# A four-layer graph network: how many columns TensorE gathers per chunk, and which memory the running sums are scanned into

## The reference

```
x += h + segment_sum(h[src] * pattern, dst) / max(deg, 1)            # layer 1
x += h + softmax attention over each node's incoming edges           # layer 2
x += segment_sum(h[src], dst) @ W                                    # layer 3
x += segment_sum(tensor product of h[src] with sh0, sh1, sh2, dst)   # layer 4
```

## Time and profile before

| | us |
|---|---|
| median of three runs | 13893.11 |
| the profiled execution | 13869.06 |
| its span, first to last instruction | 13867.2 |
| busy: PE, DVE, ACT, POOL | 11075.0, 11170.5, 3293.7, 11498.1 |
| mean granted TensorE clock | 0.895 |

### The profile page before, as it was taken

How to read it: one execution, slowest core, us unless ns; L and a number is a source line. 1 busy time by engine, 2 the same in 40 slices (tenths; PEclk the granted TensorE clock), 3 DMA queues, 4 the chain that set the end, 5 groups by cost and what they waited for, 6 DMA issues and landing times.

```text
span 13867.2 us, 198598 instructions
## 1 busy us (share of the span) xinstructions
PE 11075.0 (80%) x49235; PEld 8972.2 (65%) x49235; DVE 11170.5 (81%) x15127; ACT 3293.7 (24%) x3628; POOL 11498.1 (83%) x19996
## 2 busy tenths in 40 slices
PE   7999999991666666666569999899859999999995
PEld 6888888881545554554458888888836666666663
DVE  8988989984999999999877777777757777777775
ACT  2222222220333333333222222222201111111110
POOL 6888888887888888888778888888878888888887
PEclk9999999995777777777789999999979999999997
DMA  3323333331232322223222222222222222222221
GB/s 106 86 82 94 94 94 91 81 86 37 73 84 71 83 76 81 77 77 80 57 65 66 67 70 70 71 68 67 62 45 50 57 50 55 52 55 53 55 53 34
DMA packets 863909, 963.05 MB, mean 69 GB/s; under 512 B 426441, under 2 KB 678253, under 8 KB 863105
## 3 DMA queue, kind: packets, MB, share of 16 engines
q1 hardware_dynamic: 396088, 456.93, 12.1%
q0 software_dynamic: 327744, 170.03, 8.6%
q10 hardware_dynamic: 139400, 330.44, 6.2%
HBM read 614.57 MB, written 341.90 MB: 69 GB/s over the span
## 4 chain that ended last, share of the span: by engine, by line
issue 48%; POOL 47%; DVE 2%; POOLq 1%; PE 1%; DMA 0%; ACT 0%; SPq 0%; DVEq 0%; ACTq 0%
POOL rows L418 33%; POOL work L423 11%; POOL outs L432 2%; POOLq L422 1%; POOL q_edges L397 1%; PE psum L554 0%; PE psum L631 0%; DVE work L935 0%; DVE work L937 0%; POOLq L416 0%; PE psum L592 0%; DVE rows L767 0%; DVE h_parts L710 0%; DMA idx<-src_c 0%; DVE work L703 0%
## 5 line engine op out<-in xcount | busy, mean ns | idle before, releaser
L418 POOL DMA_INDIRECT rows<-h_table,idx x9750 | 9651.2, 990 | 2093.0 <-POOL work L423 1701.5
L554 PE MATMUL psum<-h_parts,one_hot 128*128 128x448 f32 x38808 | 8674.5, 384 | 681.4 <-ACT one_hot L461 669.9
L554 PEld LDWEIGHTS psum<-h_parts,one_hot 128*128 128x128 f32 x38808 | 7609.7, 198 | 1582.1 <-issue 790.1
L461 ACT ACTIVATE one_hot<-bit_hot 128x896 fp32r<-128x896 bf16 x2177 | 2057.8, 951 | 6984.1 <-DVE bit_hot L740 6943.8
L761 DVE TENSOR_TENSOR tile_rows<-psum,h_mask 128x448 f32<-128x448 f32 x2772 | 1721.1, 621 | 925.5 <-PE psum L554 720.9
L631 PE MATMUL psum<-work,bd_t 128*128 128x512 f32 (+1 forms) x4500 | 1766.9, 521 | 191.6 <-DVE work L1133 110.8
L767 DVE TENSOR_REDUCE rows<-tile_rows 128x32 f32<-128x448 f32 x2772 | 1694.0, 611 | 0.0
L631 PEld LDWEIGHTS psum<-work,bd_t 128*128 128x128 f32 x4500 | 823.2, 196 | 915.0 <-issue 596.9
L423 POOL MEMSET work<- 128x32 f32 x9750 | 1404.0, 144 | 3.6
L1118 DVE TENSOR_TENSOR work<-psum,work 128x800 f32<-128x800 f32 x1125 | 1102.7, 989 | 318.5 <-PE psum L622 250.0
L740 DVE TENSOR_TENSOR bit_hot<-keys,target 128x896 bf16<-128x896 int16 x2177 | 1343.6, 617 | 11.0 <-issue 11.0
(11 more groups left out here) (176 smaller groups left out, 6020.9 us busy)
## 6 DMA issues: line engine op xcount, KB each, us to landing
rows<-h_table,idx POOLq DMA_INDIRECT x9750
sums<-outs ACTq DMA_DIRECT2D x375, 400.0 KB, 2.4
dwin<-keep_rows SPq DMA_DIRECT2D x1500, 100.0 KB
attn<-outs ACTq DMA_DIRECT2D x125, 800.0 KB, 3.4
dwin<-dst_w SPq DMA_DIRECT2D x500, 100.1 KB
edge_in<-pattern_c SPq DMA_DIRECT2D x125, 400.0 KB
q_edges<-work ACTq DMA_DIRECT2D x25, 2000.0 KB
edge_in<-q_edges SPq DMA_DIRECT2D x125, 400.0 KB
```

Source lines behind the costliest of these rows:

```text
L418: nc.gpsimd.indirect_dma_start(out=rows[:, r, j * D:(j + 1) * D], out_offset=None, in_=h_table[:, :], in_offset=bass.IndirectOffsetOnAxis( ...
L461: nc.scalar.activation(one_hots[i % TILE_BUFS[l]][:, :, :], bit_hots[i % BIT_BUFS[l]], ACT.Copy).then_inc(one_hot_cast, 1)
L554: last = nc.tensor.matmul(banks[TILE_BANKS[l][b]][:, 0:H0 * D], one_hots[b][:, h1, :], h_parts[:, part, h1 * H0 * D:(h1 + 1) * H0 * D], st ...
```

## The change

Four things change. The table `PE_COLS` goes from 4 to 6 columns per chunk in the second loop, from 7, 7, 7, 7, 8 to 8 in the third and from 4, 3, 4, 3, 4 to 4 in the fourth; GpSimd's counts fall to match (2625 to 2375, 2225 to 2125, 2675 to 2625 fetches; 9750 to 9350 in all). `BIT_BUFS` is 2 for the third loop. In the first three loops the running sum whose transpose goes out is scanned into PSUM and transposed from there; in the second loop `mz` too is made in PSUM, the last element of the sum is saved in a column `o_last`, the two transposes change places, `mz_ready` is signalled by the first of them, and the two added picks stand after them; ScalarE casts their successors after it has issued the store. In the fourth loop a line picks the tiles of `ahead` beyond the fourth; with four columns there are none.

```
@@ -52,9 +52,9 @@
...
 
-PE_COLS = ((7, 7, 7, 7, 8), (4,) * RING, (7, 7, 7, 7, 8), (4, 3, 4, 3, 4))
+PE_COLS = ((7, 7, 7, 7, 8), (6,) * RING, (8,) * RING, (4,) * RING)
 PE_MAX = max(max(c) for c in PE_COLS)
-BIT_BUFS = (3, 2, 3, 2)
+BIT_BUFS = (3, 2, 2, 2)
 TILE_BUFS = (3, 2, 4, 2)
...
@@ -195,6 +195,8 @@
...
         in_ps, qh_ps = wide[0:2]
+        total_ps = wide[1]
+        o_last = sb("o_last", [P, 1])[:, :]
         acc = psum[:, 6 * 512:8 * 512].rearrange("p (a c) -> p a c", a=2)
...
@@ -504,8 +506,9 @@
...
                     nc.scalar.activation(acc_wide, mx[:, 1:CH + 1], ACT.Copy, scale=half[:, 0:1]).then_inc(mz_m_ready, 1)
-                    cast_next(1, t, r, range(2, PE_MAX))
+                    cast_next(1, t, r, range(2, 4))
                     store(1, t, r, attn_chunks, 2 * CH)
+                    cast_next(1, t, r, range(4, PE_MAX))
             for q in range(PIECES):
...
@@ -826,7 +829,7 @@
...
 
-            link(nc.vector.memset(last_of(O), 0.0))
+            link(nc.vector.memset(last_of(total_ps), 0.0))
             pick_first(0)
...
@@ -858,10 +861,10 @@
...
                     v.wait_ge(edge_used[r], t + (1 + START))
-                    then(nc.vector.tensor_tensor_scan(O, keep, in_ps, last_of(O), ALU.mult, ALU.add))
+                    then(nc.vector.tensor_tensor_scan(total_ps, keep, in_ps, last_of(total_ps), ALU.mult, ALU.add))
                     pick_next(0, t, r, range(4, 5))
                     v.wait_ge(outs_stored[r], t * 16 + (0 * TURNS * 16 + START))
-                    nc.vector.transpose(outs[:, r, 0:CH], by_edge(O)).then_inc(outs_ready[r], 1)
+                    nc.vector.transpose(outs[:, r, 0:CH], by_edge(total_ps)).then_inc(outs_ready[r], 1)
                     pick_next(0, t, r, range(5, PE_MAX))
...
@@ -968,11 +971,11 @@
...
             nc.vector.memset(mx[:, 0:1], -BIG)
-            for total in (qh_ps, Z, O):
-                link(nc.vector.memset(last_of(total), 0.0))
+            for total in (last_of(qh_ps), last_of(Z), o_last):
+                link(nc.vector.memset(total, 0.0))
             pick_first(1)
             steps1 = steps[0]
-            per_chunk1 = 7
+            per_chunk1 = 6
             with v.Fori(0, TURNS) as t:
...
@@ -1002,23 +1005,26 @@
...
                     nc.vector.tensor_tensor(acc_wide, acc_wide, nb, ALU.subtract).then_inc(rise_ready, 1)
-                    pick_next(1, t, r, range(2, PE_MAX))
+                    pick_next(1, t, r, range(2, 4))
 
...
                     then(nc.vector.tensor_tensor(in_ps, in_ps, hT, ALU.mult))
-                    then(nc.vector.tensor_tensor_scan(O, u, in_ps, last_of(O), ALU.mult, ALU.add))
+                    then(nc.vector.tensor_tensor_scan(in_ps, u, in_ps, o_last, ALU.mult, ALU.add))
 
                     v.wait_ge(mz_m_ready, n)
-                    then(nc.vector.tensor_copy(mx[:, 0:1], mx[:, CH:CH + 1]))
-                    nc.vector.scalar_tensor_tensor(out=mz, in0=Z, scalar=half[:, 1:2], in1=acc_wide, op0=ALU.mult, op1=ALU.add)\
-                        .then_inc(mz_ready, 1)
-                    v.wait_ge(mz_ready, chunk_no(0, t, r, START))
+                    nc.vector.tensor_copy(mx[:, 0:1], mx[:, CH:CH + 1])
+                    nc.vector.tensor_copy(o_last, last_of(in_ps))
+                    then(nc.vector.scalar_tensor_tensor(out=acc_wide, in0=Z, scalar=half[:, 1:2], in1=acc_wide,
+                                                        op0=ALU.mult, op1=ALU.add))
                     v.wait_ge(outs_stored[r], t * 16 + (1 * TURNS * 16 + START))
                     row = outs[:, r, :].rearrange("p (j f) -> p j f", j=J)
-                    then(nc.vector.transpose(row[:, :, 0:D], by_edge(O)))
-                    nc.vector.transpose(row[:, :, D:2 * D], by_edge(mz)).then_inc(outs_ready[r], 1)
+                    nc.vector.transpose(row[:, :, D:2 * D], by_edge(acc_wide)).then_inc(mz_ready, 1)
+                    nc.vector.transpose(row[:, :, 0:D], by_edge(in_ps)).then_inc(outs_ready[r], 1)
+                    v.wait_ge(mz_ready, chunk_no(0, t, r, START))
+                    v.wait_ge(outs_ready[r], use(1, t))
+                    pick_next(1, t, r, range(4, PE_MAX))
                     assert at[0] == per_chunk1
...
@@ -1055,13 +1061,13 @@
...
                 v.wait_ge(dwin_loaded[r], use(l, t) * (16 * G))
-                then(nc.vector.tensor_tensor_scan(O, keeps[r], messages, last_of(O), ALU.mult, ALU.add))
+                then(nc.vector.tensor_tensor_scan(acc_wide, keeps[r], messages, last_of(acc_wide), ALU.mult, ALU.add))
                 v.sem_inc(keep_used[r], 1)
                 v.wait_ge(outs_stored[r], t * 16 + (l * TURNS * 16 + START))
-                nc.vector.transpose(outs[:, r, 0:CH], by_edge(O)).then_inc(outs_ready[r], 1)
+                nc.vector.transpose(outs[:, r, 0:CH], by_edge(acc_wide)).then_inc(outs_ready[r], 1)
                 v.wait_ge(outs_ready[r], use(l, t))
 
-            link(nc.vector.memset(last_of(O), 0.0))
+            link(nc.vector.memset(last_of(acc_wide), 0.0))
             pick_first(2)
...
@@ -1124,6 +1130,8 @@
...
                     weigh(t, r, n)
+                for i in ahead[SH // 2:]:
+                    pick(3, t, i)
                 v.wait_ge(weighted_ready, t * (RING * SH) + ((r + 1) * SH + START))
...
```

7 lines of the change are left out of this document (4 added, 3 removed).

## The result

The changed kernel takes **14009.88 us** (median of four runs, 14005.89 to 14020.91) against 13894.26 for the kernel before in the same session (13877.33 to 13895.9): a ratio of 1.0087, 95% interval 1.0071 to 1.0103. It is slower, as forecast, and inside the range, but by 116 us where 61 were forecast. On some occasions every kernel, the one before too, takes 1.6 times as long (21915.19 us for the kernel before). The profiled execution took 14005.89 us; its span is 136.8 us longer than that of before.

What follows compares the result with a forecast made beforehand. GpSimd was taken to set the pace in all four loops, with VectorE very near in the second. Terms of +140, -60, -18 and -1 gave +61 us on 13893: 13954 us, range 13868 to 14100.

Steps and rivals of the forecast that it cites:

- The second loop: Second loop: VectorE's chunk becomes 28.33 us, 28.5 with waits for TensorE, against 27.35: +140 us (+90 to +227).
- 0.2 added for TensorE: Second loop: VectorE's waits for TensorE's tiles, 0 to 0.9 us per chunk, taken as 0.2.
- the term for them: Second loop: the two transposes to `outs` fall from 1.75 and 1.73 to 1.07 us, -1.34 us per chunk.
- The saved fetches: Second loop: 250 fetches fewer on GpSimd are worth nothing, only turning into waiting for free `rows` buffers.
- The third loop's: Third loop: TensorE becomes the bound at 23.4 us for eight tiles of 2.93, against 23.93: -60 us (-110 to 0).
- The fourth loop: Fourth loop: a turn of five chunks takes 138.4 us against 139.1: -18 us (-60 to +25).
- the first chunk's: Fourth loop, chunk at a turn's start: a fourth tile adds 2.93 us to 28.93, giving 31.86.
- Its shorter transpose only lengthens that wait: First loop: VectorE already waited for rows in 98 of 125 chunks, so the edit gives -1 us (-5 to 0).
- A: Rival, second loop: reading PSUM with the stride costs what SBUF costs; 29.84 us per chunk, 166 us more, 14120 us; chance 0.11.
- B: Rival, second loop: TensorE falls late at a low clock; 29.5 us per chunk, +124, 14078 us; chance 0.10.
- C: Rival, third and fourth loops: GpSimd's pace holds, 22.97 and 136.6 us, -113 and -60; kernel 13810 or 13860 us; chance 0.17.
- the signs listed: Changed profile: PSUM transposes 1.0 to 1.1 us, second loop 28.1 to 28.9 without row waits, GpSimd waiting there for VectorE.

Runs made afterwards that it cites:

- pad61_c: The changed kernel with 61 empty semaphore increments on VectorE ahead of the second loop, nothing else: 13870.4 us, ratio to the kernel before 0.9977.
- l2_four_d: The changed kernel with four columns by TensorE in the second loop again instead of six: 13739.06 us, ratio to the kernel before 0.989.
- best_d: The changed kernel with four columns in loop 2, first sum in SBUF, 60 and 50 idle GpSimd instructions ahead of loops 1 and 3: 13656.12 us, ratio 0.9839.

## Why the prediction had the sign right and the size wrong

| loop | forecast | measured | with VectorE's code loaded (pad61_c) |
|---|---|---|---|
| first | -1 | +44.1 | +37.5 |
| second | +140 | +165.6 | +117.9 |
| third | -60 | -22.3 | -118.6 |
| fourth | -18 | -50.6 | -53.5 |

The last column is made as the others, from first and last starts against the earlier trace rows, as 3509.1 - 3391.2 in the second loop. It splits the loss: loading costs 48 us in the second loop and 96 in the third. The 96 is good to some 20 us only, because TensorE's own pace varies: the third loop took 23.15 us for every chunk in l2_four_d and 22.90 in best_d, with no loading and no stop of TensorE in either, 31 us apart over the loop. Why it does so is open. The gaps themselves, 24 x (27.18 - 22.93), are 102 us.

**The step that failed** is the one that was not there. The prediction took every period as a chunk's work, and counted the instructions it added as durations only, never as code. The trace had the warning: the earlier trace rows shows 3.52 us at the start of a turn in which VectorE waits for nothing that the trace names. I took it up as a price peculiar to the fourth loop and kept it, instead of asking what it was and whether the other loops, whose bodies the change makes longer, would get it. The loading is some 144 us in all, more than the whole loss of 136.8.

**The second loop**, code apart, went by its steps. The transposes that read PSUM:

```profile
L1023 DVE STREAM_TRANSPOSE outs<-psum x125: 1016/1016/1020, 3521.4 to 7078.1; 128x800 f32<-128x800 f32 x125
```

```profile
L1024 DVE STREAM_TRANSPOSE outs<-psum x125: 972/973/976, 3522.4 to 7079.0; 128x800 f32<-128x800 f32 x125
```

They take 1.02 and 0.97 us (L867 1.005), against 1.07 forecast and the 1.73 and 1.75 of the earlier trace rows; the copy of `o_last` takes 0.15. VectorE never waits for rows after the first chunk and sets the pace at 28.30 us with its code loaded, where 28.33 was worked out and 0.2 added for TensorE. The transposes took 0.15 us less than the term for them, and TensorE's tiles cost 16.4 us in the whole loop, 0.13 a chunk: 28.33 - 0.15 + 0.13 = 28.31. The saved fetches were worth nothing, as the forecast said.

**The third loop's** term was mis-sized the other way. I took 2.93 us a tile from 98 matmuls and 23.4 for eight; the 393 above give 80.51 / 393 x 14 = 2.87 and 22.94, which is what the earlier trace rows had shown in one interval (22.97). -118.6 of pad61_c stands against a lower end of -110. The loading took 96 of it back.

**The fourth loop.** A turn takes 5 x 27.41 = 137.0 us where 138.4 was forecast. (The upper end of that forecast is summed wrongly: 4 x 26.9 + 31.86 = 139.5 gives +9, not +25.) The step that was off is the first chunk's: the fourth tile was to add 2.93 us to its 28.93; it takes 137.0 - 4 x 26.7 = 30.2, so it added 1.3: some of TensorE's extra tile runs in the gap of 75.8 / 22 = 3.4 us in which VectorE waits for code. With the code loaded (pad61_c) the turn is no shorter, 136.9: GpSimd sets it then, at the 136.6 that the forecast named as its pace, and VectorE waits for rows in 76 of 124 chunks instead of 10. A stall of VectorE is free where GpSimd is as slow.

**The first loop.** "Its shorter transpose only lengthens that wait" was true of VectorE and false of the kernel: 98 waits for rows meant that GpSimd was the bound, and a bound can be made slower by what runs beside it. About 20 to 30 of the 44 us are this edit's; the other 15 to 25 are partly scatter (the kernel before repeated to 0.08 us a chunk, 10 us) and partly open.

**The rivals.** A, the dear read of PSUM, fell with the 1.02 and 0.97 us; the sentence of the Trainium skill, "PSUM — Partial Sum Buffer", Specifications, on non-contiguous patterns does not carry over to VectorE's transposes. Where the prediction says that the rows agree with the 1.7 ns per column of the Trainium skill, "Vector Engine (DVE) Microarchitecture Reference", section 5.2, they do so in direction only: an estimate by that figure is 1.36 us for 800 columns, and the row has 1.74. B, a late TensorE, fell as well: the granted clock rose to 0.91, and the waits for tiles stayed at 0.13 us a chunk. C named both mechanisms of the later loops rightly, GpSimd's or TensorE's pace near 22.93 and 136.6, and pad61_c has them; the second loop, at 28.30 and not 28.1, and the first, at +37.5 and not -1, kept the sum from being 13810, and the loading hid it. Of the signs listed, the third loop's 23.1 to 23.6 and the fourth's 27.6 to 27.8 came out at 23.75 and 27.41. L1024 is just under its 1.0 us, and GpSimd's wait in the second loop (466.8 us, 46 times, up to 21.1) has no releaser in the trace, so that it can't be read off that it is VectorE for which GpSimd waits. The others came out as written.

## What to carry to other kernels

Count the instructions of a written-out loop body on each engine, not only their time, and look at the packets of the instruction queue per turn: a wait without a releaser, once per turn, on the first instructions of the body was code being loaded here, and a change that lengthens any body moves all that follow it. The wait alone does not show it: moving the code and counting the packets does. Before a change is dropped as slower, shift its code by half a block; here 61 idle instructions were worth 1.1%, more than the whole change. And where an engine only waits for another, making it faster need not be free: the one that it waits for can be stretched.

## What was not expected of the hardware

A body of VectorE of 266 to 326 instructions ran without a fetch when, by the fitted rule, it touched three blocks of 128, and cost 2.2 to 3.9 us per turn when it touched four: 51.8 / 24 at L990, 92.6 / 24 at L1086, 75.8 / 22 in the fourth loop. The same holds for GpSimd, at 2.3 to 3.0 us in the first loop. Why the third loop's gap is nearly twice the second's is open. So is why TensorE's same stream of matmuls, without a stop and at a granted clock of 1.00, gives a chunk in 23.15 us in one run and 22.90 in another. One fetch of GpSimd per chunk lasts until 2.65 us after the start of VectorE's compare of 128x3200 bf16, 1.67 or 1.97 us where most take 0.95. A strided read of PSUM by VectorE's transpose runs at the pace of a strided write (1.02 and 0.97 us for 128x800), while the same transpose between two SBUF tiles takes 1.68 to 1.79 us.
